# Another list of store slots for a batched pairwise-product kernel: 65 slots in place of 64, the last five stores issued by ScalarE

## The chip, the cores and the metric

The kernel runs on one core of one Trainium2 chip. The metric is the device time of one execution in microseconds, as the median of three runs. VectorE (DVE) multiplies, TensorE (PE) does a small matrix product, and SyncE (SP) and ScalarE (ACT) do nothing but issue DMA transfers and pass semaphores on. GpSimd does no work.

## The reference

For each of 4096 batch rows there are 32 field vectors of 64 numbers (float32). Every field vector is multiplied by one 64 x 64 matrix W, and for each of the 496 pairs i < j the field i is multiplied, element by element, with the transformed field j:

```python
def _L0_rec_ref(x, W):
    NUM_FIELDS = 32
    EMBED_DIM = 64
    BATCH = 4096
    vid = jnp.einsum('bfd,de->bfe', x, W)
    F_ = x.shape[1]
    idx_i, idx_j = jnp.triu_indices(F_, k=1)
    return x[:, idx_i, :] * vid[:, idx_j, :]
```

The input is 4096 x 32 x 64 and the output 4096 x 496 x 64 numbers, so the output is 15.5 times as large as the input.

## The kernel before

The batch is cut into 16 tiles (`NT`). A unit is one field, or one product of a pair, of a tile: 128 partitions x 128 columns of float32, that is 64 KB. One SBUF tensor, `mem`, has 446 units (`UNITS`). It holds the fields of the loaded tiles as well as the products that wait for their store. `vid` is PSUM: the 32 transformed fields of one tile, four to a bank.

Per tile, TensorE makes `vid` in two halves of four banks; ScalarE lets each half start (semaphore `go`) when its fields have landed and VectorE has done with the banks. VectorE then makes the 496 products of the tile in a fixed order (`by_block`), as multiplications of many units at once. Every multiplication adds one to the semaphore `dve`. The 16 x 496 = 7936 products follow each other in one sequence, and this sequence is cut into **slots**. `SLOTS` lists them in order: a slot has a size in units (its sign says whether it is filled upward or downward) and a first unit in `mem`. A multiplication ends where a slot ends; `CUTS` says where else one is cut in two, by the units from the start of a slot. So the list decides three things: where in `mem` each product goes, how long each multiplication is, and how large each store is.

When the last multiplication of a slot has been put down, the slot's store is queued, one DMA for the whole slot. The engine that issues it, SyncE for the first `SP_SLOTS` slots and ScalarE for the rest, waits for a count of `dve`. For all slots but the first this is the number of the slot's last multiplication. For the first slot it is one more:

```python
q = sp if slot < SP_SLOTS else act
q.after_products(done + (slot == 0))
s = sem(f"s{slot}")
q.engine.dma_start(out[:, begin : begin + size, :], mem[:, lo : lo + size, :]).then_inc(s, 16)
```

`after_products(n)` is a wait until `dve` has reached n. Here `done` counts the multiplications so far, the one just added included. A multiplication that writes units on which an earlier store is still reading waits for that store's semaphore (`s0`, `s1`, ...).

The input comes in three stretches. ScalarE issues the first one at the start, in four loads: W with the first half of tile 0 (`x0`), the second half of tile 0, and tiles 1 to 5 in two parts (`HEAD`). The other two stretches (`STRETCHES`, tiles 6 to 10 and 11 to 15) are issued by SyncE behind slots 23 and 43 (`LOAD_BEHIND`), in the same queue as the stores. Transfers that one engine issues run one after the other; those of SyncE (queue q1) and of ScalarE (queue q10) can run at the same time.

Of the kernel before, what the change touches and what calls it, by code (L numbers as in the profile page):

```python
# [39 lines left out]
FRESH = [tiles[0] for tiles, _ in STRETCHES]  # L40

SLOTS = [
# [9 lines left out]
]  # L52
CUTS = {
# [5 lines left out]
}  # L59
LOAD_BEHIND = [23, 43]  # L60

SP_SLOTS = len(SLOTS) - 4

PAD = 24
PAD0 = 8
# [131 lines left out]
def build(nc, x0, x, out):  # L197
# [73 lines left out]
    for t in range(NT):  # L271
# [10 lines left out]
        for pos, m, n, i, di, j, dj in products(t, ENDS):  # L282
# [33 lines left out]
            if pos + m * n == begin + size:  # L316
                if held is not None:
                    nc.sync.wait_ge(*held)
                    held = None
                q = sp if slot < SP_SLOTS else act  # L320
                q.after_products(done + (slot == 0))
# [72 lines left out]
```

## Time and profile before

| | |
|---|---|
| median of 3 runs | 1284.18 us (1283.57 to 1284.43) |
| profiled execution, its own time | 1283.99 us |
| its span, first to last instruction | 1282.7 us |
| moved by DMA | 553.73 MB, mean 432 GB/s over the span |
| VectorE busy | 1077.8 us (84%), 255 multiplications |
| TensorE busy | 166.0 us (13%) |
| transfers that SyncE issues | 64 (60 stores, 4 loads) |
| transfers that ScalarE issues | 8 (4 loads, 4 stores) |

The span is the time between the first and the last instruction; the profiled execution's own time is 1.3 us more than that. The DMA engines move data over nearly all of the span, and VectorE is the only other engine with much to do. In the views a rate in a short stretch is uneven, since data is counted packet by packet and the packets of the 16 DMA engines end nearly together; stretches of some tens of microseconds can be compared.

### The profile page before, as it was taken

How to read it: one execution, taken by the hardware profiler on the slowest of the kernel's cores; microseconds unless marked ns; L12 is line 12 of the kernel's file. 1: busy time of each engine (PE TensorE's matmuls, PEld its weight loads, DVE VectorE, ACT ScalarE, POOL GpSimd, SP SyncE). 2: the span in 40 equal slices, each digit the busy share in tenths (PEclk: the TensorE clock that was granted, in tenths of full speed). 3: DMA queues.
4: the chain of work that ended last, by engine and by line, in shares of the span. 5: the costliest groups of instructions: out<-in, count | busy, mean ns of one | idle time of the engine just before them, and what ended most of it. 6: DMA issues, size and time to landing. Idle time of an engine off the chain costs nothing. (4 is left out here: it accounts for less than half of the span.)

```text
span 1282.7 us, 1107 instructions
## 1 busy us (share of the span) xinstructions
PE 166.0 (13%) x256; PEld 65.1 (5%) x256; DVE 1077.8 (84%) x255; POOL 0.2 (0%) x4
## 2 busy tenths in 40 slices
PE   2030110303010020030301203002020020302000
PEld 1010000101000000010100001001000000101000
DVE  6799998989889647889999979918899898999582
POOL 0000000000000000000000000000000000000000
PEclk8565565656556556575655556556555565657555
DMA  9999999999999999999999999999999999999999
GB/s 391 433 439 435 429 437 442 429 425 441 441 425 431 439 429 433 425 446 437 425 435 443 429 425 441 436 422 433 426 431 446 429 427 446 435 427 425 448 433 394
DMA packets 10370, 553.73 MB, mean 432 GB/s; under 512 B 1152, under 2 KB 1152, under 8 KB 1152
## 3 DMA queue, kind: packets, MB, share of 16 engines
q1 hardware_dynamic: 9216, 508.56, 91.6%
q10 hardware_dynamic: 1152, 45.15, 8.3%
q14 instruction: 2, 0.02, 0.0%
HBM read 33.62 MB, written 520.09 MB: 432 GB/s over the span
## 5 line engine op out<-in xcount | busy, mean ns | idle before, releaser
L194 DVE TENSOR_TENSOR mem<-mem,vid 128x2048 f32<-128x2048 f32 (+13 forms) x255 | 1077.8, 4296 | 181.6 <-DMA out_dram<-mem 151.7
L255 PE MATMUL vid<-mem 128*128 (+1 forms) x256 | 166.0, 811 | 1010.6 <-PEq L254 1010.6
L255 PEld LDWEIGHTS vid<-mem 128*128 128x128 f32 x256 | 65.1, 267 | 1110.6 <-issue 1110.6
L362 POOL MEMSET const-bfloat16-1.0<- 128x1 bf16 x1 | 0.1, 103 | 0.0
L362 POOL MEMSET const-uint8-127<- 128x1 uint8 x1 | 0.1, 102 | 0.0
L362 POOL MEMSET const-float32-0.0<- 128x1 f32 x1 | 0.1, 100 | 0.2 <-issue 0.2
L362 POOL MEMSET const-float32-1.0<- 128x1 f32 x1 | 0.1, 99 | 0.0
## 6 DMA issues: line engine op xcount, KB each, us to landing
out_dram<-mem SPq DMA_DIRECT2D x7, 7168.0 KB, 21.0
out_dram<-mem SPq DMA_DIRECT2D x4, 6144.0 KB, 20.9
mem<-in_r_x_dram SPq DMA_DIRECT2D x2, 7936.0 KB, 38.7
mem<-in_r_x_dram ACTq DMA_DIRECT2D x1, 7936.0 KB, 25.9
out_dram<-mem ACTq DMA_DIRECT2D x1, 7168.0 KB, 37.9
mem<-in_r_x_dram SPq DMA_DIRECT2D x2, 2304.0 KB, 44.0
mem<-in_r_x_dram ACTq DMA_DIRECT2D x1, 2304.0 KB, 36.9
mem<-in_L_rec_W_x_dram ACTq DMA_DIRECT2D x1, 1088.0 KB, 5.6
```

The lines of the kernel that those rows point to most:

```text
L194: self.engine.tensor_tensor(*operands, MULT).then_inc(self.dve, 1)
L255: nc.tensor.matmul(vid[:, b * BANK : b * BANK + BANK, :], lhsT=w, rhs=mem[:, bass.ds(k * step + (first + b * BANK), BANK), :], start=True, ...
L362: nc = _bacc.Bacc("TRN2", target_bir_lowering=False, num_devices=1, dynamic_dma_scratch_size=256)
```

## The change

The list `SLOTS` is replaced by another one, with 65 slots of again 7936 units in all, and so is `CUTS`. ScalarE issues the last five stores in place of four. Nothing else changes. Of the two tables the diff shows the first lines:

```diff
 SLOTS = [
-    (96, 32), (96, 190), (-128, 62), (96, 190), (96, 32), (112, 128), (112, 0), (-128, 158),
+    (112, 32), (128, 144), (112, 32), (-80, 206), (-64, 142), (-112, 17), (-128, 129), (128,
...
 CUTS = {
-    1: (32,), 2: (62,), 4: (24,), 6: (32,), 7: (44,), 8: (16,), 9: (16,), 10: (32,), 12:
+    3: (14,), 4: (56,), 6: (48,), 8: (16, 29), 9: (24,), 10: (16,), 11: (28,), 12: (16,),
...
-SP_SLOTS = len(SLOTS) - 4
+SP_SLOTS = len(SLOTS) - 5
```

**VectorE at the start of the program.** These are its first multiplications before the change, with the elements that each writes per partition (128 to a unit) and the semaphores that it waits for:

```order
L194 TENSOR_TENSOR mem<-mem,vid 128x8192 [waits barrier_Pool_Activation_PE_DVE_SP_release,pe]
L194 TENSOR_TENSOR mem<-mem,vid 128x2048
L194 TENSOR_TENSOR mem<-mem,vid 128x2048 [waits pe]
L194 TENSOR_TENSOR mem<-mem,vid 128x4096 [waits pe]
L194 TENSOR_TENSOR mem<-mem,vid 128x8192
L194 TENSOR_TENSOR mem<-mem,vid 128x4096
L194 TENSOR_TENSOR mem<-mem,vid 128x2048 [waits pe]
L194 TENSOR_TENSOR mem<-mem,vid 128x1792
L194 TENSOR_TENSOR mem<-mem,vid 128x256 [waits s0]
```

And these are the first ones of the changed kernel:

```order
L193 TENSOR_TENSOR mem<-mem,vid 128x8192 [waits barrier_Pool_Activation_PE_DVE_SP_release,pe]
L193 TENSOR_TENSOR mem<-mem,vid 128x2048
L193 TENSOR_TENSOR mem<-mem,vid 128x2048 [waits pe] x2
L193 TENSOR_TENSOR mem<-mem,vid 128x14336
L193 TENSOR_TENSOR mem<-mem,vid 128x2048 [waits pe]
L193 TENSOR_TENSOR mem<-mem,vid 128x2048 [waits s0]
L193 TENSOR_TENSOR mem<-mem,vid 128x2048 x3
L193 TENSOR_TENSOR mem<-mem,vid 128x6144
L193 TENSOR_TENSOR mem<-mem,vid 128x1792
L193 TENSOR_TENSOR mem<-mem,vid 128x256 [waits s1]
```

The first slot grew from 96 to 112 units, so it takes four multiplications in place of three, and the one behind it, which the first store waits for as well, is now one of 112 units (14336 elements) in place of one of 32 (4096). The second slot is filled by the fifth and the sixth multiplication, and the third slot begins with the one that waits for `s0`.

**SyncE at the start of the program**, with the size of each transfer per partition, before the change:

```order
L323 DMA out_dram<-mem 128x12288 [waits barrier_Pool_Activation_PE_DVE_SP_release,dve]
L323 DMA out_dram<-mem 128x12288 [waits dve]
L323 DMA out_dram<-mem 128x16384 [waits dve]
L323 DMA out_dram<-mem 128x12288 [waits dve] x2
L323 DMA out_dram<-mem 128x14336 [waits dve] x2
```

And in the changed kernel:

```order
L322 DMA out_dram<-mem 128x14336 [waits barrier_Pool_Activation_PE_DVE_SP_release,dve]
L322 DMA out_dram<-mem 128x16384 [waits dve]
L322 DMA out_dram<-mem 128x14336 [waits dve]
L322 DMA out_dram<-mem 128x10240 [waits dve]
L322 DMA out_dram<-mem 128x8192 [waits dve]
```

The first three stores are larger by 16, 32 and -16 units. By the code, SyncE's first store waited for `dve` to reach 4 and now waits for 5, and the second waits for 6 in place of 5.

**ScalarE at the end of the program.** Before the change, from the last of its loads on:

```order
L219 DMA mem<-in_r_x_dram 128x4608
L323 DMA out_dram<-mem 128x16384 [waits x0,h0,h1,dve,h2,g23_0,g23_1,g43_0,g43_1]
L323 DMA out_dram<-mem 128x14336 [waits dve]
L323 DMA out_dram<-mem 128x16384 [waits dve] x2
L342 ISA [waits s61,s62,s40,s20]
```

In the changed kernel:

```order
L218 DMA mem<-in_r_x_dram 128x4608
L322 DMA out_dram<-mem 128x14336 [waits x0,h0,h1,dve,h2,g23_0,g23_1,g43_0,g43_1]
L322 DMA out_dram<-mem 128x16384 [waits dve]
L322 DMA out_dram<-mem 128x14336 [waits dve]
L322 DMA out_dram<-mem 128x16384 [waits dve] x2
L341 ISA [waits s62,s63,s40,s21]
```

One store of 112 units now stands ahead of the four that were there, in the queue of ScalarE, beside the last one of SyncE.

## Rows read from the trace of the kernel before

**Rows 1.** The page: busy time by engine, and all that DMA moved.

```profile
PE 166.0 (13%) x256; PEld 65.1 (5%) x256; DVE 1077.8 (84%) x255; POOL 0.2 (0%) x4
DMA packets 10370, 553.73 MB, mean 432 GB/s; under 512 B 1152, under 2 KB 1152, under 8 KB 1152
```

**Rows 2.** Stretches: length, busy times by engine, granted clock, DMA share, GB/s.

```profile
0.00:27.00 27.00, 9.04 (x16) 3.75 (x16) 16.74 (x4) 0.20 (x4) 0.88 0.94 395
27.00:40.00 13.00, 0.00 (x0) 0.00 (x0) 13.00 (x3) 0.00 (x0) 0.50 1.03 405
0.00:60.00 60.00, 9.04 (x16) 3.75 (x16) 43.68 (x13) 0.20 (x4) 0.67 0.98 410
60.00:440.00 380.00, 54.50 (x80) 21.30 (x80) 339.21 (x80) 0.00 (x0) 0.57 1.00 435
440.00:480.00 40.00, 6.15 (x10) 2.75 (x11) 21.54 (x4) 0.00 (x0) 0.53 0.99 425
480.00:840.00 360.00, 47.00 (x72) 18.11 (x70) 318.65 (x77) 0.00 (x0) 0.57 1.00 433
840.00:890.00 50.00, 8.57 (x16) 3.56 (x16) 23.37 (x5) 0.00 (x0) 0.56 1.02 431
890.00:1190.00 300.00, 40.74 (x64) 15.61 (x64) 281.46 (x69) 0.00 (x0) 0.58 1.00 434
1240.00:1250.00 10.00, 0.00 (x0) 0.00 (x0) 10.00 (x3) 0.00 (x0) 0.50 0.94 406
```

**Rows 3.** Who waited for whom: total us, times, longest.

```profile
DVE mem L194 <- DMA out_dram<-mem: 151.7, 32, 28.2
```

**Rows 4.** Timeline of the start: start us, length, instruction, count (merged).

```profile
0.72 0.38 ACTq L219 DMA_DIRECT2D mem<-in_L_rec_W_x_dram  x1
...
10.26 34.47 DVE L194 TENSOR_TENSOR mem<-mem,vid 128x8192 f32<-128x8192 f32 x8 [10.26 <-PE vid L255]
...
18.86 8.81 DVE L194 TENSOR_TENSOR mem<-mem,vid 128x2048 f32<-128x2048 f32 x3
...
21.06 15.21 DVE L194 TENSOR_TENSOR mem<-mem,vid 128x2048 f32<-128x2048 f32 x3
...
27.70 0.37 SPq L323 DMA_DIRECT2D out_dram<-mem  x1
```

**Rows 5.** Multiplications by size, whole run: count, busy us, mean ns.

```profile
L194 DVE TENSOR_TENSOR mem<-mem,vid 128x2048 f32<-128x2048 f32 x135 | 301.2, 2278 | 30.5 <-DMA out_dram<-mem 30.5
...
L194 DVE TENSOR_TENSOR mem<-mem,vid 128x6144 f32<-128x6144 f32 x21 | 137.4, 6546 | 19.3 <-PE vid L255 14.2 <-DMA out_dram<-mem 5.0
...
L194 DVE TENSOR_TENSOR mem<-mem,vid 128x14336 f32<-128x14336 f32 x4 | 60.3, 15087 | 24.3 <-DMA out_dram<-mem 24.3
```

**Rows 6.** DMA up to 30 us: packets, MB, share; then KB and issue to landing.

```profile
q10 hardware_dynamic: 523, 11.97, 95.0%
...
mem<-in_r_x_dram ACTq DMA_DIRECT2D x1, 7936.0 KB, 25.9
...
mem<-in_r_x_dram ACTq DMA_DIRECT2D x1, 2304.0 KB, 36.9
mem<-in_L_rec_W_x_dram ACTq DMA_DIRECT2D x1, 1088.0 KB, 5.6
mem<-in_r_x_dram ACTq DMA_DIRECT2D x1, 1024.0 KB, 7.6
```

**Rows 7.** The chain that ended last, one piece of it: a store of 8192 KB.

```profile
1015.76 22.99 DMA out_dram<-mem
```

**Rows 8.** Timeline of ScalarE's stores near the end: start us, length.

```profile
1206.07 0.35 ACTq L323 DMA_DIRECT2D out_dram<-mem  x1
...
1242.21 0.34 ACTq L323 DMA_DIRECT2D out_dram<-mem  x1
```

**Rows 9.** The page, DMA issues of ScalarE's stores: KB, us to landing.

```profile
out_dram<-mem ACTq DMA_DIRECT2D x1, 7168.0 KB, 37.9
```

23 rows, old and new, of tables (CUTS, SLOTS) are left out of this document.

## The prediction

> **What bounds the kernel now.** I read the page first, then the rate of DMA stretch by stretch, and only then the waits. The page says that 553.73 MB are moved in a span of 1282.7 us, while VectorE is busy for 1077.8 us [rows 1]. The stretches say what the transfers can do at most: 435 GB/s for 380 us on end, 433 and 434 in the two other long ones [rows 2]. At 434 GB/s the 553.73 MB take 1275.9 us. So the DMA engines stand still, or run below that rate, for only 1282.7 - 1275.9 = 6.8 us in all, and the kernel is bound by them. VectorE's 151.7 us of waits for stores [rows 3] cost nothing by themselves: it waits for room in SBUF, and while it waits the queue is moving data.
>
> This gives the rule for everything below: time is lost only where no transfer is ready, and what is lost there can't be won back later, because the rate is already at its top. No change of the list can gain more than these 6.8 us, and the bytes are the same.
>
> Where do the 6.8 us lie? In the first 27 us the rate is 395 GB/s [rows 2], that is 10.67 MB, which take 24.6 us at 434; so 2.4 us go before data flows. ScalarE issues the first load at 0.72 us [rows 4], so **from an issue into an empty queue to the flow of data it is 2.4 - 0.7 = 1.7 us**. Up to 60 us, at 410 GB/s, 3.3 us are lost, 0.9 us more; the stretch from 27 to 40 us at 405 GB/s says the same (13 x 29/434 = 0.9) [rows 2]. That is the place where the loads of the start end and the first store begins. The two stretches with the later loads lose 0.8 us (425 GB/s over 40 us) and 0.3 us (431 over 50 us), and the ten microseconds around 1245 us, at 406 GB/s, lose 0.65 us [rows 2]. The remaining 1.6 us are spread over the run and the end.
>
> **The change, part by part.**
>
> *The first store.* Before, its wait is for four multiplications. The timeline shows them: the first from 10.26 to 18.86 us, the second to 21.06, so one of 2048 elements takes 2.20 us on the path, and the store goes out at 27.70 us, as the one of 4096 elements ends [rows 4]. After, five have to end: 8192, three times 2048, and then 14336 elements, which took 15.09 us in the run before [rows 5]. Nothing among them waits for a store, and TensorE's 16 products of the first tile lie within the first 27 us [rows 2]. So the fifth ends at 18.86 + 3 x 2.20 + 15.09 = 40.6 us. The store is issued **12.9 us later than before**.
>
> What runs until then? Only the four loads of the start: 7936 + 2304 + 1088 + 1024 KB = 12.65 MB [rows 6]. Of these 11.97 MB had landed at 30 us; the other 0.68 MB take 1.6 us at 434 GB/s, so the loads are through at 31.6 us. (2.4 us and 29.1 us for 12.65 MB give the same.) After that both queues are empty: SyncE's stores stand behind the first in order, and ScalarE has nothing to issue before its stores at the end. The flow starts again at 40.6 + 1.7 = 42.3 us. **The hole is 42.3 - 31.6 = 10.7 us.** The 1.7 us are measured on a load and not on a store; the bounds are nothing (hole 9.0 us) and what the smallest load shows, 5.6 us to landing less 2.6 us for its 1.11 MB, 3.0 us (hole 12.0 us) [rows 6]. I take 1.7, since it is also an issue into an empty queue and leaves the landing out. The 0.9 us that before loses at the same place are in the hole already. Net: 10.7 - 0.9 = +9.8 us (8.1 to 11.1).
>
> *The next stores.* The second slot needs only one more multiplication of 2048 elements and is ready at 42.8 us, while the first store is just beginning; no loss. The third slot lies where the first one was, so it waits for the first store to land, and then has four multiplications of 2048 and one of 6144: 4 x 2.28 + 6.55 = 15.7 us [rows 5]. Meanwhile the second store, 8192 KB or 8.39 MB, takes 19.3 us. So the third store is issued 3.6 us before the second lands. Is that enough? One store of the run before took 22.99 us from issue to landing [rows 7]; less 19.3 us of its own this is 3.7 us spent behind the store ahead, and its stretch ran at 434 GB/s [rows 2]. A store that was too late is near the end: ScalarE's one of 7168 KB, issued at 1206.07 and landing 37.9 us later, at 1244.0, has its successor issued at 1242.21 [rows 8, 9], 1.8 us ahead, and there the 0.65 us are lost. So 3.6 us cost nothing, and 1.8 us would cost well under a microsecond. Being ahead by more than that, which the other stores may now be, gains nothing either.
>
> *The later loads* are the same transfers, again one slot's store ahead of what needs them; I keep their 0.8 and 0.3 us (bounds: nothing, and twice that).
>
> *One more store.* At 435 GB/s and a DMA share of 1.00 over 380 us [rows 2], some 20 stores in a row leave no gap that shows; an error of 1 GB/s would be 0.9 us, or 0.04 us each. I put the 65th at 0.0 us. The Trainium skill speaks against it: SBUF — State Buffer, "The DMA setup-cost knee", has every transfer pay a roughly fixed 2 us whatever its size. By that the 65th would add 2.0 us and the sum below would come to 1295.3 us; for stores that are queued while another one runs the trace does not agree, since 20 of them would lose 40 of the 380 us.
>
> *The end.* ScalarE gets a store of 112 units more, ahead of the same last three sizes: 7168 KB, 16.9 us of data that lie in its queue while VectorE fills the last slots. The loss around 1245 us should go: -0.5 us (bounds: 0, if VectorE is held up by the same stores, and -0.65).
>
> *VectorE's other work* is 249 multiplications over the same elements, in place of 255. It is covered by the 200 us that VectorE is idle; without that cover, 6 fewer are worth less than a microsecond.
>
> **Sum:** +9.8 + 0.0 - 0.5 = +9.3 us. Against the profiled execution's own 1283.99 us this is **1293.3 us**, or 0.7% slower. (The median of the three runs is 0.2 us above that execution, which is far inside the bounds.)
>
> **The rivals.** What a measurement of this kernel can tell from no change is about 0.2%, 2.6 us, from 1281.6 to 1286.8 us.
>
> A, *the loads cover the wait* (not slower). The last load of the start took 36.9 us from issue to landing [rows 6]; issued by 2.1 us, it landed at about 39 us. If that were its own pace, the queue would run until 39 and the hole be 42.3 - 39.0 = 3.3 us; 3.3 - 0.9 - 0.5 = +1.9 us, 1285.9 us, no change that can be told. It decides from an end of the loads at 38 us on. Against it: the 11.97 MB at 30 us, and that from 27.70 us on the first store shared the engines with this load. Chance 4 in 100.
>
> B, *the gain that more time ahead would give, without the hole* (faster). It would need the first store to go out with its own four multiplications, at 25.5 us. Then the 0.9, 0.65 and, at best, the 0.8 and 0.3 us would all go: 2.65 us, 1281.3 us. Against it stands the wait for one more multiplication in the code. Chance 2 in 100, and 1 more for a gain that no view shows.
>
> C, *the hole, and late stores behind it.* The new list is run from a start 9 us later against the same loads, and if the third store or some like it are issued less than 2 us ahead, each loses 0.65 us or more; four or five make +3 us, 1296.3 us. For it: 3.6 us is a margin of only 1.8 us. Against it: room and stores move together, because VectorE waits for the stores. Chance 10 in 100.
>
> **How the numbers follow.** The forecast has 83 in 100, A 4, B and its like 3, C 10. Slower by over 0.2%: 0.93; within: 0.04; faster: 0.03. The range: the hole's bounds give 1291.6 to 1294.6 us around the forecast; the dips of the later loads, gone or doubled, widen this by 1.1 us on either side, and the end by up to 0.5 us above. 1290.5 to 1296.0 holds the forecast's cases and the nearer half of C.
>
> **What would show it.** In the changed kernel's profile: SyncE's first store at 40.6 us; next to no DMA from 32 to 41 us; VectorE's first wait for a store ending at about 60 us; 434 GB/s in the long stretches from 60 us on; no dip some 40 us before the end. I would be wrong if the first store were issued near 28 us, if the DMA engines were busy until 38 us, or if the rate fell to under 430 GB/s in a stretch without loads, which would be C.

## The result, and the profile after

The changed kernel takes 1294.20 us (median of 6 runs, 1293.97 to 1294.85), the kernel before 1284.16 us (6 runs). The ratio is 1.0079, with a 95% interval of 1.0068 to 1.0090: **0.8% slower, 10.0 us.** The profiled execution of the changed kernel has a span of 1292.9 us, 10.2 us more than before.

The page of the changed kernel has the same bytes and nearly the same busy times as [rows 1]. The line of rates (40 equal slices of the span, here 32.3 us each) has its low value in the second slice:

```profile
PE 162.8 (13%) x256; PEld 63.6 (5%) x256; DVE 1077.4 (83%) x249; POOL 0.2 (0%) x4
...
GB/s 391 324 430 450 418 442 432 424 452 424 434 440 424 430 414 452 432 421 446 422 450 426 422 452 424 434 432 430 422 454 414 432 452 422 436 440 418 453 426 391
DMA packets 10514, 553.73 MB, mean 428 GB/s; under 512 B 1168, under 2 KB 1168, under 8 KB 1168
```

Stretches of the changed kernel (length, busy times, granted clock, DMA share, GB/s), to be read beside [rows 2]:

```profile
27.00:40.00 13.00, 0.00 (x0) 0.00 (x0) 13.00 (x1) 0.00 (x0) 0.50 0.34 147
32.00:41.00 9.00, 0.00 (x0) 0.00 (x0) 9.00 (x2) 0.00 (x0) 0.50 0.00 0
41.10:41.20 0.10, 0.00 (x0) 0.00 (x0) 0.10 (x1) 0.00 (x0) 0.50 10.77 4588
0.00:60.00 60.00, 9.65 (x16) 3.90 (x16) 33.79 (x7) 0.20 (x4) 0.65 0.82 351
60.00:440.00 380.00, 52.85 (x80) 20.32 (x80) 342.43 (x85) 0.00 (x0) 0.57 1.00 433
440.00:480.00 40.00, 1.62 (x2) 0.84 (x3) 27.82 (x4) 0.00 (x0) 0.50 0.99 419
840.00:890.00 50.00, 4.12 (x5) 1.85 (x6) 24.14 (x4) 0.00 (x0) 0.50 1.02 434
890.00:1190.00 300.00, 41.63 (x66) 16.29 (x65) 269.34 (x59) 0.00 (x0) 0.58 1.00 434
1240.00:1250.00 10.00, 0.00 (x0) 0.00 (x0) 10.00 (x3) 0.00 (x0) 0.50 0.88 378
1250.00:1260.00 10.00, 0.00 (x0) 0.00 (x0) 10.00 (x2) 0.00 (x0) 0.50 1.15 498
```

From 32 to 41 us the DMA share is 0.00, while VectorE is busy for all of the nine microseconds. The first packets of the first store begin at 41.1 us (a packet is counted whole where it begins, so a share can be over 1). The timeline of the changed kernel has the two ends of it: the first store's issue (merged with the second, which stands right behind it), and VectorE's first wait for that store, beside [rows 4]. The last row is the issue of the next loads, which waits for the store of slot 21 to land:

```profile
40.27 2.54 SPq L322 DMA_DIRECT2D out_dram<-mem  x2
...
58.69 4.48 DVE L193 TENSOR_TENSOR mem<-mem,vid 128x2048 f32<-128x2048 f32 x2 [16.25 <-DMA out_dram<-mem]
...
441.59 1.64 SPq L218 DMA_DIRECT2D mem<-in_r_x_dram  x2
```

The DMA view of the changed kernel up to 41 us shows that the loads of the start, all 12.65 MB, were the only thing moved, and that the last one of them landed 30.6 us after its issue, where it took 36.9 us beside the first store [rows 6]:

```profile
q10 hardware_dynamic: 576, 12.65, 73.0%
...
out_dram<-mem SPq DMA_DIRECT2D x1, 7168.0 KB, 18.4
mem<-in_r_x_dram ACTq DMA_DIRECT2D x1, 2304.0 KB, 30.6
```

### The profile page after: what moved, and what is told of

It is laid out like the page before. It is cut to its first block and busy times, and to the rows that moved or that the text cites. A ratio compares the mean times of both kernels' runs of the same rounds, so it can differ in the third digit from the quotient of the medians.

```text
span 1292.9 us, 1103 instructions
## 1 busy us (share of the span) xinstructions
PE 162.8 (13%) x256; PEld 63.6 (5%) x256; DVE 1077.4 (83%) x249; POOL 0.2 (0%) x4
## 5 line engine op out<-in xcount | busy, mean ns | idle before, releaser
L193 DVE TENSOR_TENSOR mem<-mem,vid 128x2048 f32<-128x2048 f32 (+11 forms) x249 | 1077.4, 4398 | 184.0 <-DMA out_dram<-mem 145.3
L254 PE MATMUL vid<-mem 128*128 (+1 forms) x256 | 162.8, 797 | 1031.7 <-PEq L253 1031.7
## 6 DMA issues: line engine op xcount, KB each, us to landing
out_dram<-mem SPq DMA_DIRECT2D x2, 4096.0 KB, 24.6
```

The costliest lines, as they stand in the source:

```text
L193: self.engine.tensor_tensor(*operands, MULT).then_inc(self.dve, 1)
L254: nc.tensor.matmul(vid[:, b * BANK : b * BANK + BANK, :], lhsT=w, rhs=mem[:, bass.ds(k * step + (first + b * BANK), BANK), :], start=True, ...
```

## The experiments

Theory H: the loss is the hole ahead of the first store, and the hole comes from that store's wait for a fifth, long multiplication. Theory L: the new list itself loses time, by late stores or slower transfers. Times are medians, and each ratio is to the kernel before on the same chip.

| run | first store issued | time, us | ratio (95%) |
|---|---|---|---|
| new list, own wait | 25.70 us | 1284.72 | 1.0006 (0.9997 to 1.0015) |
| old list, wait for six | 40.39 us | 1294.02 | 1.0078 (1.0064 to 1.0092) |
| new list, cut at 32 units | 29.92 us | 1284.12 | 1.0000 (0.9991 to 1.0009) |
| new list, own wait, four stores on ScalarE | 25.14 us | 1284.99 | 1.0008 (0.9999 to 1.0017) |
| old list, wait for five | 36.04 us | 1289.84 | 1.0043 (1.0027 to 1.0058) |
| old list, cut at 48 units | 29.59 us | 1284.09 | 0.9998 (0.9989 to 1.0007) |
| the same, five stores on ScalarE | 29.96 us | 1284.12 | 0.9999 (0.9990 to 1.0008) |
| the same, loads on ScalarE | 29.81 us | 1308.27 | 1.0188 (1.0174 to 1.0202) |
| new list, cut at 32, loads on ScalarE | 29.45 us | 1301.87 | 1.0138 (1.0123 to 1.0154) |

**1. The new list, with the first store waiting for its own slot only.**

```diff
-                q.after_products(done + (slot == 0))
+                q.after_products(done)
```

> The changed kernel with one thing undone: the first store waits for its own four multiplications, not for the fifth. Theory H (the hole ahead of the first store is the whole loss): the first store goes out at 25.5 us, the DMA engines are busy from 2 us on, and the time is that of the kernel before or up to 1 us less, 1283.2 to 1284.2 us. Theory L (the new list itself loses time, by late stores or by slower transfers): the first store goes out at 25.5 us as well, but only about 8 us of the 10 come back, 1286 us, and the rate from 60 to 440 us stays at 433 GB/s or less.

Measured: 1284.72 us, 9.5 us of the 10.0 are gone. It is 0.6 us above the kernel before, which the interval can't tell from nothing, and 0.5 us above the range that theory H gave. The timeline of this run, for the first two stores and VectorE's first wait, and the issue of the next loads:

```profile
25.70 17.53 SPq L322 DMA_DIRECT2D out_dram<-mem  x2
...
50.99 15.35 DVE L193 TENSOR_TENSOR mem<-mem,vid 128x2048 f32<-128x2048 f32 x5 [8.13 <-DMA out_dram<-mem]
...
432.56 1.66 SPq L218 DMA_DIRECT2D mem<-in_r_x_dram  x2
```

What follows: the loss hangs on when the first store may go, not on the 64 slots behind it. Theory L's 1286 us are not there. Its other sign is, 433 GB/s from 60 to 440 us (435 before), but next to nothing was lost with it.

**2. The old list, with a first store as late as that of the changed kernel.**

```diff
-                q.after_products(done + (slot == 0))
+                q.after_products(done + 3 * (slot == 0))
```

> The kernel before with its old list, whose first store waits for six multiplications in place of four. The sixth ends at 40.7 us by the timeline of the run before, where the changed kernel issues its first store at 40.3 us. Theory H: the same hole with the old list costs the same, 1293.5 to 1294.5 us. Theory L: the hole costs 8 us, 1292 us, and the 2 us that the changed kernel lost beside it don't show here. If the rate from 60 to 440 us falls from 435 to 433 GB/s here too, the slower rate belongs to the hole and not to the list.

Measured: 1294.02 us, as slow as the changed kernel. The timeline of this run:

```profile
40.39 0.85 SPq L323 DMA_DIRECT2D out_dram<-mem  x2
...
56.38 7.01 DVE L194 TENSOR_TENSOR mem<-mem,vid 128x256 f32<-128x256 f32 x4 [11.89 <-DMA out_dram<-mem]
...
444.11 1.64 SPq L219 DMA_DIRECT2D mem<-in_r_x_dram  x2
```

What follows: the hole alone, without anything else of the change, makes the whole of the 10 us. Runs 1 and 2 together settle H against L. The rate from 60 to 440 us is 433 GB/s here, as with the new list without a hole (run 1), so it doesn't say whether the slower rate belongs to the hole or to the list. That needs a finer measure, below.

**3. The new list with one more cut**, so that the fifth multiplication, for which the first store still waits, has 32 units in place of 112.

```diff
 CUTS = {
+    1: (32,),
     3: (14,), 4: (56,), 6: (48,), 8: (16, 29), 9: (24,), 10: (16,), 11: (28,), 12: (16,),
```

> The changed kernel with one more cut: the fifth multiplication is split after 32 units, into 4096 and 10240 elements, so that the first store, with its wait for five as it is, goes out at 25.5 + 4.4 = 29.9 us, 2 us before the loads of the start end. Theory H: no hole, the time of the kernel before or up to 1.5 us less, 1282.7 to 1284.2 us. Theory L: about 1286 us.

Measured: 1284.12 us, the time of the kernel before. The timeline of this run:

```profile
29.92 13.27 SPq L322 DMA_DIRECT2D out_dram<-mem  x2
...
50.02 15.35 DVE L193 TENSOR_TENSOR mem<-mem,vid 128x2048 f32<-128x2048 f32 x5 [7.20 <-DMA out_dram<-mem]
...
431.70 1.64 SPq L218 DMA_DIRECT2D mem<-in_r_x_dram  x2
```

So one number in the table, with the rule for the first store as it is, is enough to close the hole. The store also goes out 4.2 us later than in run 1 and lands 1.0 us earlier (50.02 against 50.99 us): ahead of the end of the loads, an earlier issue is no gain.

**4. Four stores on ScalarE in place of five**, on top of run 1 (`SP_SLOTS = len(SLOTS) - 4`).

> As the run with the first store's own wait, and ScalarE issues four stores in place of five, with the new list. If the fifth store on ScalarE is what removes the loss of some 0.4 us near the end, this run is slower than that one by 0.4 us; if the new list removes it, or neither, the two agree within 0.3 us.

Measured: 1284.99 us against 1284.72; the two agree within 0.3 us, in runs that spread over 1.6 us. The fifth store on ScalarE is worth nothing that can be told.

**5. The old list with a hole of half the length**: as run 2, with `2 * (slot == 0)`.

> The kernel before with its old list, whose first store waits for five multiplications, which end at 36.3 us, 4.1 us ahead of the run that waited for six. If each microsecond of the hole costs one, the time is 1294.0 - 4.1 = 1289.9 us. Theory K (any stretch in which all DMA engines stand idle makes the transfers behind it slower): from the landing of the first store to the issue of the next loads it takes 1.3 us longer than in the kernel before, as in the run with six. Rival: that loss grows with the hole, then it is about 0.7 us here and the time 1289.3 us. If the hole were not the cause, the time would not follow the issue.

Measured: 1289.84 us, for an expected 1289.9. The first store goes out 4.35 us earlier than in run 2 and the time is 4.2 us less: **a microsecond of hole costs a microsecond.** The timeline of this run:

```profile
36.04 0.85 SPq L323 DMA_DIRECT2D out_dram<-mem  x2
...
52.04 9.21 DVE L194 TENSOR_TENSOR mem<-mem,vid 128x256 f32<-128x256 f32 x5 [7.57 <-DMA out_dram<-mem]
...
439.74 1.64 SPq L219 DMA_DIRECT2D mem<-in_r_x_dram  x2
```

These timelines also give the finer measure. Between VectorE's first wait for a store, which ends as slot 0's store lands, and the issue of the next loads, which waits for slot 21's, the stores of slots 1 to 21 are moved and nothing else: 2560 units in the old list, 2528 in the new one. In the kernel before, and then in runs 7 and 4, the two marks are these:

```profile
48.78 9.21 DVE L194 TENSOR_TENSOR mem<-mem,vid 128x256 f32<-128x256 f32 x5 [4.05 <-DMA out_dram<-mem]
...
435.19 1.63 SPq L219 DMA_DIRECT2D mem<-in_r_x_dram  x2
```

```profile
47.67 9.21 DVE L194 TENSOR_TENSOR mem<-mem,vid 128x256 f32<-128x256 f32 x5 [2.82 <-DMA out_dram<-mem]
...
434.08 1.63 SPq L219 DMA_DIRECT2D mem<-in_r_x_dram  x2
```

```profile
50.78 15.35 DVE L193 TENSOR_TENSOR mem<-mem,vid 128x2048 f32<-128x2048 f32 x5 [8.48 <-DMA out_dram<-mem]
...
432.38 1.65 SPq L218 DMA_DIRECT2D mem<-in_r_x_dram  x2
```

| list | hole | between the marks, us |
|---|---|---|
| old | none (kernel before) | 435.19 - 48.78 = 386.41 |
| old | none (run 6, below) | 434.35 - 47.43 = 386.92 |
| old | none (run 7) | 434.08 - 47.67 = 386.41 |
| old | wait for five | 439.74 - 52.04 = 387.70 |
| old | wait for six | 444.11 - 56.38 = 387.73 |
| new | none (run 1) | 432.56 - 50.99 = 381.57 |
| new | none (run 3) | 431.70 - 50.02 = 381.68 |
| new | none (run 4) | 432.38 - 50.78 = 381.60 |
| new | changed kernel | 441.59 - 58.69 = 382.90 |

Each row is one profiled execution, and those of the old list without a hole differ by 0.5 us. Behind a hole the same transfers take 0.8 to 1.3 us longer, in both lists and after a short hole as after a long one. That fits theory K of run 5; its rival, a loss that grows with the hole, is out. That idle engines are the cause, and not something else that goes with a late first store, is not shown.

**6 and 7. The old list with the first store at 29.9 us**, and then with five stores on ScalarE as well (`SP_SLOTS = len(SLOTS) - 5`).

```diff
-    1: (32,), 2: (62,), 4: (24,), 6: (32,), 7: (44,), 8: (16,), 9: (16,), 10: (32,), 12:
+    1: (48,), 2: (62,), 4: (24,), 6: (32,), 7: (44,), 8: (16,), 9: (16,), 10: (32,), 12:
```

> The kernel before with its old list and one cut moved: the fourth multiplication has 48 units in place of 32, so that the first store, with its wait for four, goes out at 29.9 us in place of 27.7. In the run of the new list with a first store at 29.9 us no rate was lost between the loads and the first store. If those 0.9 us are won here and stay won, 1283.2 us. Rival: the later loads give them back, 1284.1 us, as in that run of the new list, whose time was that of the kernel before.

> As the run with the moved cut, and ScalarE issues the last five stores in place of four, with the old list. The third store from the end is then issued 4 us before the one ahead lands, in place of 1.8 us. If the 0.4 us near the end are lost to that short lead, this run is 0.4 us faster than the one with the moved cut alone; if the lead of 1.8 us cost nothing, the two agree.

Measured: 1284.09 and 1284.12 us. Neither beats the kernel before. The timeline of run 6 shows where the gain went; the last row is the issue of the second later stretch of loads:

```profile
29.59 6.80 SPq L323 DMA_DIRECT2D out_dram<-mem  x2
...
47.43 9.21 DVE L194 TENSOR_TENSOR mem<-mem,vid 128x256 f32<-128x256 f32 x5 [2.95 <-DMA out_dram<-mem]
...
434.35 1.66 SPq L219 DMA_DIRECT2D mem<-in_r_x_dram  x2
...
841.83 1.64 SPq L219 DMA_DIRECT2D mem<-in_r_x_dram  x2
```

The first store lands 1.35 us earlier than before, the first later loads are issued 0.84 us earlier, and the second ones, at 841.73 us before and 841.83 us here, no earlier at all. By this one trace of each, the start is won and **given back by the time of the second loads**; of that, 0.9 us go between the two issues of loads. Why that stretch is shortest in the kernel before (406.54 us; 407.48 in run 6, and 407.7 to 408.3 in the other three traces of the old list) was not found out; it can be chance of that one execution. The step from four stores on ScalarE to five gained nothing in this list either.

**8 and 9. The later loads on ScalarE's queue**, on top of run 7 and of run 3, to take the turn from a store to a load out of one queue.

```diff
-                    sp.after(stored[-2])
-                    stretch(sp, tiles, runs, f"g{slot}_")
+                    act.after(stored[-2])
+                    stretch(act, tiles, runs, f"g{slot}_")
```

> The old list with the moved cut and five stores on ScalarE, and the two later stretches of loads issued by ScalarE in place of SyncE, after the same waits, so that they run beside the store that is under way and not behind it. If the 1 to 1.5 us that are lost where a load follows a store in one queue come from that change of direction, they go at both loads, and the time is about 1282 us. Rival: the loss follows the loads into the other queue, 1284.1 us, as in the run with five stores; if the shared store now lands later and holds VectorE up, 1285 us or more.

> The new list with the cut of 32 units, and its two later stretches of loads issued by ScalarE in place of SyncE. By the first theory about 1282 us here too, 2 us under the run with the cut alone; by the rival 1284.1 us.

Measured: 1308.27 and 1301.87 us, far from 1282 and from 1284.1 us. Only the last clause of run 8's expectation, a shared store that lands later and holds VectorE up, went this way; it put it at 1285 us or more. Rows of run 8's profile say why. First come the stretches around the first later loads:

```profile
440.00:480.00 40.00, 0.00 (x0) 0.00 (x0) 17.54 (x3) 0.00 (x0) 0.50 0.93 394
...
480.00:490.00 10.00, 7.17 (x13) 3.22 (x14) 4.41 (x2) 0.00 (x0) 0.71 0.43 184
```

VectorE's wait for the store that was under way, in run 7 and then in run 8:

```profile
453.80 10.88 DVE L194 TENSOR_TENSOR mem<-mem,vid 128x2048 f32<-128x2048 f32 x2 [4.63 <-DMA out_dram<-mem]
```

```profile
471.59 10.88 DVE L194 TENSOR_TENSOR mem<-mem,vid 128x2048 f32<-128x2048 f32 x2 [22.46 <-DMA out_dram<-mem]
```

VectorE's waits of run 8 from 430 to 500 us, and around the second later loads, from 830 to 920 us:

```profile
DVE mem L194 <- DMA out_dram<-mem: 32.6, 2, 22.5
...
DVE mem L194 <- DMA out_dram<-mem: 47.1, 1, 47.1
```

Both queues are served at once, so the store under way is slowed by the load beside it; VectorE waits 22.5 us for it in place of 4.6, the first store behind the loads comes late, and the rate falls to 184 GB/s. At the second loads the wait is 47.1 us, where the longest before was 28.2 [rows 3]. Run 9 shows the same, with 164 GB/s from 470 to 480 us. It is a hole once more, made in another way. ScalarE also lets TensorE start, but that did not come late: VectorE's waits for TensorE are 24.6 us in all in run 8, and 29.9 us in the kernel before. Whether the turn from store to load costs the missing microsecond stays open.

## Why the prediction was right, step by step

**What bounds the kernel** was right: with VectorE idle for 200 us, 9 us without transfers were never won back (runs 2 and 5).

**The first store** was right in its mechanism and its place: issue at 40.27 us for 40.6, nothing moved from 32 to 41 us, the loads alone in the queue. Its size was off. Run 6, whose first store is queued before the loads end, has the first store landed at 47.43 us. The changed kernel has it at 58.69 us, of which 2.4 us are the 16 units more that its first slot holds (1.05 MB at 434 GB/s): the hole is worth 58.69 - 2.4 - 47.43 = 8.9 us and not 10.7. The step that failed is the price of 1.7 us from an issue to the flow, taken from a load. The first packets of the store begin at 41.1 us, 0.9 us after its issue. It landed 18.4 us after the issue, of which its 7168 KB take 16.9 us, so start and landing together are 1.5 us. The rest of the miss lies in the issue, 0.3 us earlier than forecast, and in loads that ended a little after the 31.6 us of the sum. What before loses at the same place was put too low, at 0.9 us; run 6 gives 48.78 - 47.43 = 1.35 us. Net, the start cost 7.5 us and not 9.8.

**What was missing** makes up for it. The sum put nothing on the stretches behind the hole. There the changed kernel loses 1.2 us up to the first later loads (382.90 us against 381.57 to 381.68 for the same list), and from there to the end it takes 1292.9 - 441.59 = 851.3 us, where before took 847.5; it has 16 units more to move in that part, 2.4 us, which leaves 1.4 us. So the span's 10.2 us are 7.5 + 1.2 + 1.4 within rounding. The 1.4 us are not the hole's: run 3, the same list without a hole and with a span of 1282.9 us, takes 1282.9 - 431.70 = 851.2 us there. Beside run 3 the hole costs 58.69 - 50.02 = 8.7 us at the start, 1.2 us up to the first later loads and 0.1 us behind them, which is the whole difference of the two spans, 10.0 us. The 1.4 us may be no more than a low 847.5: the other four traces of the old list have 848.1 to 849.4 us there. The total of the forecast, +9.3, was close by luck, because errors ran against each other.

**The end**, -0.5 us, was not there. The 406 GB/s from 1240 to 1250 us [rows 2] were read as a loss of 0.65 us, and the changed kernel, whose stores are issued well ahead, has 378 GB/s in those ten microseconds and 498 in the next ten. A stretch of ten microseconds is too short for such a reading, since the 16 engines' packets of 64 KB end in bunches of 1 MB, a quarter of what ten microseconds hold. Runs 4 and 7 agree that the fifth store gains nothing.

**The third store** was right. In the changed kernel it is issued 4.0 us before the second lands, for 3.6 forecast; these are its issue and the end of VectorE's wait for the second (`s1`):

```profile
74.06 0.33 SPq L322 DMA_DIRECT2D out_dram<-mem  x1
...
78.09 16.55 DVE L193 TENSOR_TENSOR mem<-mem,vid 128x256 f32<-128x256 f32 x3 [2.12 <-DMA out_dram<-mem]
```

It and those like it cost nothing that can be told: with the hole closed, the new list is level with the old one (run 3).

**One more store** at nothing fits runs 3 and 6: 65 and 64 stores, both without a loss at the start, 1284.12 and 1284.09 us. The roughly 2 us for each transfer that the Trainium skill states (SBUF — State Buffer, "The DMA setup-cost knee") do not appear for stores that are queued behind another one.

**The rivals.** A fell with the last load landing 30.6 us after its issue, once it no longer shared the engines with a store. B's time, 1281.3 us, was not reached by any run with an early first store, run 1 among them, which meets B's condition: what can be won at the start was not kept. C did not happen: the long stretches ran at 433 and 434 GB/s.

## What to carry to other kernels

In a kernel that its transfers bound, read a new plan first at the places where the queue can be empty: the start, and any transfer that waits for one more thing than its own data. A wait for "the next operation" has no fixed price; here the same line cost 4.4 us with one list and 15.1 us with another. And a stall that is taken away counts only when the end moves: the first store of run 6 landed 1.35 us earlier, and the kernel ended no earlier.

## What the runs showed of the hardware that was not expected

After a stretch in which all DMA engines stood idle, some 20 stores in a row took 0.8 to 1.3 us longer (387.7 us for 386.4 to 386.9; 382.9 for 381.6 to 381.7), whether the first store had been issued at 36 or at 40 us. One more thing goes with it in the packets of the traces. In the three runs with such a hole the 16 engines end slot 0's store within 0.2 us of each other; in the six without one that are in the table above they end it 0.95 to 1.25 us apart. The mark of a landing is that of the last engine, so part of the difference comes from how it is measured: by the mean of the 16 engines it is 0.7 to 1.0 us. Why the rest is lost is not shown by these runs.
